# Edge loop of a graph network: VectorE forms the remainder of both message tiles in one operation, and GpSimd issues gathers only

## The reference

```python
edge_feat = concatenate([x[src], x[dst], edge_attr])        # 20000 x 1088
h        = mish(edge_feat @ W1 + b1)                        # 20000 x 512
messages = mish(h @ W2 + b2)                                # 20000 x 512
agg      = segment_sum(messages, dst, num_segments=1250)
```

## Time and profile before

| | |
|---|---|
| time, median of 3 runs | 1254.94 us (1253.52 to 1257.24) |
| the profiled execution | 1255.11 us, span 1253.5 us |
| PE busy in the span | 1084.6 us, 87% |
| DVE busy | 958.0 us, 76% |
| ACT busy | 837.7 us, 67% |
| POOL busy | 713.5 us, 57% |

### The profile page before, as it was taken

The page is one execution under the profiler, slowest core; times in us unless marked ns, Lnnn a source line. Parts: engine busy times, 40 slices in busy tenths (PEclk is TensorE's granted clock), DMA queues, the critical chain, the costliest instruction groups (busy, mean ns, idle before and its releaser), DMA issues. The chain is left out here.

```text
span 1253.5 us, 19768 instructions
## 1 busy us (share of the span) xinstructions
PE 1084.6 (87%) x5651; PEld 884.2 (71%) x5652; DVE 958.0 (76%) x1678; ACT 837.7 (67%) x1025; POOL 713.5 (57%) x574
## 2 busy tenths in 40 slices
PE   3993999999999999999999999996389985668974
PEld 2772788787778778878777877885267764658862
DVE  6651799898989989989989999998548875733366
ACT  3212889989988998998998988897045441523342
POOL 3246777777777777787877777752111210644420
PEclk9995999999999999999999999998589995779985
DMA  6826666666666666666666666660011112624445
GB/s 167 276 89 153 143 121 130 125 125 125 129 126 122 127 128 121 129 126 123 129 125 126 124 126 129 119 149 1 23 46 42 33 58 82 205 76 127 134 130 179
DMA packets 129763, 148.72 MB, mean 119 GB/s; under 512 B 73253, under 2 KB 81862, under 8 KB 129597
## 3 DMA queue, kind: packets, MB, share of 16 engines
q0 software_dynamic: 39280, 97.61, 36.2%
q1 hardware_dynamic: 90381, 50.03, 15.1%
q10 hardware_dynamic: 16, 0.02, 0.0%
HBM read 137.02 MB, written 15.69 MB: 122 GB/s over the span
## 5 line engine op out<-in xcount | busy, mean ns | idle before, releaser
L907 PE MATMUL ps<-W2h,w1l_w3l 128*128 128x512 f32 x1264 | 426.6, 398 | 0.0
L778 POOL DMA_INDIRECT gath<-dst_table,idx_sl x158 | 265.2, 1679 | 48.6 <-issue 47.1
L771 POOL DMA_INDIRECT gath<-src_table,idx_sl x158 | 207.9, 1316 | 126.1 <-PE ps L902 86.0
L907 PEld LDWEIGHTS ps<-W2h,w1l_w3l 128*128 128x128 f32 x1264 | 227.3, 189 | 38.6
L907 PE MATMUL ps<-W2l,w1l_w3l 128*128 128x512 f32 x632 | 248.2, 393 | 0.0
L845 DVE TENSOR_TENSOR agg<-agg,ps 125x512 f32 x166 | 114.0, 687 | 76.5 <-issue 47.7
L785 POOL TENSOR_TENSOR msg_lo<-act,msg_hi 128x512 fp32r<-128x512 f32 x79 | 144.2, 1825 | 35.3 <-DVE msg_hi L891 35.3
L907 PEld LDWEIGHTS ps<-W2l,w1l_w3l 128*128 128x128 f32 x632 | 119.0, 188 | 27.2
L802 ACT ACTIVATE act<-ps 128x1024 f32<-128x1024 f32 x79 | 81.2, 1027 | 74.8 <-PE ps L939 74.8
L902 PE MATMUL ps<-ident,gath 128*128 128x128 f32 x632 | 99.0, 282 | 34.8 <-DVE agg L845 18.4
L902 PEld LDWEIGHTS ps<-ident,gath 128*128 128x128 f32 x632 | 73.6, 142 | 62.5 <-DVE agg L845 35.3
(11 more groups left out here) (324 smaller groups left out, 2391.7 us busy)
## 6 DMA issues: line engine op xcount, KB each, us to landing
f_w_raw<-in_L_ffn_w_dram SPq DMA_DIRECT2D x32, 512.0 KB, 4.7
ea_sl<-ea_scr SPq DMA_DIRECT2D x158, 64.0 KB, 3.2
ea_scr<-in_edge_attr_dram POOLq DMA_DIRECT2D x1, 5000.0 KB
w_raw<-in_L_gnn_W_dram SPq DMA_DIRECT2D x3, 1024.0 KB, 12.6
gath<-src_table,idx_sl POOLq DMA_INDIRECT x158
gath<-dst_table,idx_sl POOLq DMA_INDIRECT x158, 5.1
x_raw<-in_x_dram SPq DMA_DIRECT2D x5, 448.0 KB
src_table<-tabs SPq DMA_DIRECT2D x10, 224.0 KB
```

The source lines that it names most:

```text
L771: pool.indirect_dma_start(out=gath[:, k, j, :], out_offset=None, in_=src_table[:, :], in_offset=bass.IndirectOffsetOnAxis(ap=idx_sl[:, p % ...
L778: pool.indirect_dma_start(out=gath[:, k, j, :], out_offset=None, in_=dst_table[:, :], in_offset=bass.IndirectOffsetOnAxis(ap=idx_sl[:, p % ...
L907: return nc.tensor.matmul(ps_2[:, p % 2, j, :], part[:, p % 2, d, j * P:(j + 1) * P], weights[:, d, :], start=False, stop=last)
```

## The change

VectorE's L867 covers both tiles of the pair (128 x 1024 instead of 128 x 512). GpSimd's subtraction (L785) and its two waits are gone, and two semaphores become one, so ScalarE and TensorE have one wait less each.

```diff
@@ gpsimd
-                p = s - 4
-                if exists(p):
-                    pool.wait_ge(S["msg_hi_ready"], p + 1)
-                    need(pool, S["sum_ps"], ring_free(p))
-                    nc.gpsimd.tensor_tensor(msg_lo[:, ring(p)][:, 1], act2[:, p % A2, 1], f32(msg_hi[:, ring(p)][:, 1]), ALU.subtract).then_inc(S["msg_lo1_ready"], 1)
@@ scalar
-                        act.wait_ge(S["msg_lo0_ready"], g - A2 + 1)
-                        act.wait_ge(S["msg_lo1_ready"], g - A2 + 1)
+                        act.wait_ge(S["msg_lo_ready"], g - A2 + 1)
@@ vector
-                    nc.vector.tensor_tensor(msg_lo[:, ring(m)][:, 0], a4[:, 0], f32(msg_hi[:, ring(m)][:, 0]), ALU.subtract).then_inc(S["msg_lo0_ready"], 1)
+                    nc.vector.tensor_tensor(msg_lo[:, ring(m)], a4, f32(msg_hi[:, ring(m)]), ALU.subtract).then_inc(S["msg_lo_ready"], 1)
@@ tensor
-                    pe.wait_ge(S["msg_lo0_ready"], min(m + 1, PAIRS))
-                    pe.wait_ge(S["msg_lo1_ready"], min(m + 1, PAIRS))
+                    pe.wait_ge(S["msg_lo_ready"], min(m + 1, PAIRS))
```

More of the change, by code:

```diff
@@ L713, in edge_phase @@
         names = ("eaT_ps eaT_hi eaT_lo gath_read lin1_ps exp1 inc1 sq1 ln1 quot1 h_ready h_hi h_lo lin2_ps "
-                 "exp2 inc2 sq2 ln2 quot2 msg_ready msg_hi_ready msg_lo0_ready msg_lo1_ready onehot_ready sum_ps summed w3_in w3_hi w3_lo").split()
+                 "exp2 inc2 sq2 ln2 quot2 msg_ready msg_hi_ready msg_lo_ready onehot_ready sum_ps summed w3_in w3_hi w3_lo").split()
         S = {n: sem("e_" + n) for n in names}
```

## The result

| | before | after |
|---|---|---|
| time, median of 4 runs | 1254.51 us (1253.52 to 1257.24) | 1226.41 us (1225.22 to 1227.05) |
| profiled execution, span | 1253.5 us | 1224.3 us |
| ratio after to before | | 0.9771, 95% interval 0.9754 to 0.9789 |

28 us or 2.3% faster. 1251.5 was forecast, with a range from 1229 to 1268, whose lower end the result misses by 2.6 us. The time is near that of rival A, 1229, but not by rival A's way.

What follows compares the result with a forecast made beforehand. Bound: a per-step ring of 9.46 us through VectorE's register load, held by the adding gather. Sum: 1255.1 - 2.8 (shorter ring) - 1 (last steps) = 1251.3, taken as 1251.5 us; range 1229 to 1268.

Steps and rivals of the forecast that it cites:

- rival A: On GpSimd, first dst gather starts ahead of L879, takes 1.57; load comes later and is free; 1229 us, chance 0.22.
- The held register load: VectorE's load L840 before tile 1's addition takes 1060 ns, not about 310, while the adding gather is on its way.
- the ring: Closed chain each step: bank end, src gathers, first dst gather, load, addition, transposes, bank end; 9.46 us, forecast 9.42.
- the ring law: Step period is first dst gather's end after bank end, plus 2.38, plus 1.40: 5.68 + 3.78 = 9.46 us.
- What moves the gathers: On GpSimd: first src gather 0.44 shorter, first dst gather starts at 3.66; -0.04 us a step, -2.8 us.
- The third gather's length: First dst gather on GpSimd, begun just behind VectorE's L879, takes 2.02 us instead of 1.57 and ends at 5.67.
- rival C: First src gather not shortened or dst gather held longer, ending at 6.12; 1285 us, half of it 1270; chance 0.09.
- The price of 0 for GpSimd's subtraction: Removing L785 moves no gather: 0 us, although GpSimd is busy 148 us less.
- VectorE's part: Doubled L867 adds 0.53 us a step on VectorE, hidden with some 0.35 to spare; 42 us if paid in full.
- TensorE's wait for L875: PE's L910 waits for VectorE's L875 by about 0.1 us each step, with 0.5 to give.
- The last steps: From about 855 us, L785 no longer holds L862, but L867's +0.53 is paid; between -3 and +3, taken as -1.

Runs made afterwards that it cites:

- e3_one_input: Kernel before plus a VectorE reduction (128 x 512, one SBUF input, constant tile) behind L867, GpSimd's subtraction kept: 1270.18 us.
- e8_sub_first: Kernel after with the wide VectorE subtraction moved ahead of L857, so that it ends before the first src gather starts: 1249.62 us.
- e2_pool_to_spare: Kernel after with GpSimd's subtraction put back, its result written to a spare tile that nobody reads: 1259.98 us.
- e1_pool_left_out: Kernel before without GpSimd's subtraction, TensorE multiplying msg_hi in both places, VectorE keeping its 128 x 512 form: 1254.69 us.

## Why the prediction was wrong

**Right: what bounds the kernel.** The held register load and the ring through it stand. Moving the load alone gives the 30 us, and the ring law (end of the first dst gather + 3.74 to 3.78) gives the period of the kernel before, of e3_one_input (9.65) and of e8_sub_first (5.67 + 3.74 = 9.41). It was fitted to the kernel before; the other two are independent of it. Its tacit condition is that the load comes into the transfer; in the kernel after it does not.

**The step that failed: "What moves the gathers", its first term.** I wrote that the first src gather "gets 0.44 shorter" since the CAST moves behind its end. It got 0.41 longer. The 1.43 of before was laid to the CAST L872. e3_one_input shows that it belongs to the subtraction L867, which begins 0.12 ahead of the gather and ends inside it. I took both for explanations of the same 1.43, as the two operations stand back to back. But two rows of before could have separated them. The second src gather of each step (1.29, with L879 beginning 0.48 into it) shows what an operation at the CAST's place gives. And the gather of 0.99 in the earlier trace rows, which I called one with no CAST over it, had L872 (from 613.60 on) over its last 0.33 us and was no longer for it. Made 0.53 longer, L867 holds the gather that much longer: 0.99 + 0.97 - 0.11 = 1.85 against 1.84 measured (from 0.24 ahead to 0.97 inside). The dst gather thus moves from 4.11 to 4.53 instead of to 3.66.

**The third gather's length failed too.** The prediction has it at 2.02 by L879, which stands ahead of it. At 4.53 that operation is over; the gather is lengthened by L887 or L891 (now L881 and L885), which begin after it. No term of the prediction has these two. Without them the gather would end at 6.1 and the load at 6.7 would be held, as in the three steps of 9.60 to 9.65: 70 such steps would have made the kernel slower than before, by some 10 us (an estimate, 70 x (9.63 - 9.48), as if each of these steps could follow another). With them it ends at 6.5 or 7.1 and the load is ahead of its transfer. That is luck: 0.15 us in the start of L881 (1.22 or 1.37 into the gather) decides.

**The rule that I set aside.** I weighed the rule of the Trainium skill (SBUF — State Buffer, Who interferes with whom) that a VectorE operation with two SBUF inputs contends with a GpSimd instruction that reads SBUF. I threw it out by one row, a gather of 0.99 under L867. In that row the gather starts at 612.94 and L867 at 613.00: the gather was first. The same section says that who issues first gets the ports; e2_pool_to_spare shows both orders in one trace, 0.99 with the gather 0.05 ahead and 1.95 with it 0.14 behind. I used that rule for rival A and not for this row. I also drew the wrong end from it: a held gather was priced as a longer ring, +45 us, and put under C with a chance of 0.02, when with the later and longer dst gather the load escapes and the ring opens.

**The price of 0 for GpSimd's subtraction.** It is right for the schedule of before (e1_pool_left_out) and wrong for that of after (e2_pool_to_spare), where L785 would end past the bank end and stand in front of the next gather. "It would cost or give something only where the gathers stood behind it" names the condition; I did not put the new times into it.

**A slip in rival C.** Its 6.12 holds the third gather by L879 at its present place, 4.11. By the prediction's own formula only 0.11 of L879 is left there, which costs nothing, so a first gather that is merely not shortened would have left the ring at 9.46.

**Rival A** has the right consequence, the load free and VectorE's own work as the period, 9.1 forecast and 9.09 measured. Its cause, the gather ahead of L879 and the load after the transfer, is not what happened.

**VectorE's part.** +0.53 is exact (L861 1.22). It was forecast hidden with 0.35 to spare; with the ring gone it is the bound. TensorE's wait for L875 (0.1 forecast) came as 0.26 for the weight load; the matmuls on the two sides of L910 start 0.08 further apart than before (0.55 against 0.47), so the forecast holds for the matmuls. The last steps, forecast at -1, gave +0.2 (from the 76th bank end to the last addition 83.1 us before, 83.3 after). The sum: -1.0 up to the sixth bank end, 70 x (9.095 - 9.479) = -26.9, +0.2, and -1.5 in the phases that the change does not touch: -29.2, the difference of the two spans.

## What to carry to other kernels

When an engine idles on its own queue, look at each register load by itself: its duration can depend on the DMA under way, and moving it to a quiet place (0.3 instead of 1.07 us, 1224.5 us here) got what this change got by accident; the two are not apart by their intervals. When two operations stand back to back in front of a slow one, a row does not say which of them holds it; and a row that shows no interference counts only if the order of start is the one in question. How long such an instruction takes counts as much as when it starts: with the short dst gather the same later start gave steps of 9.6. In a loop that closes on itself, an edit must be priced on the schedule it makes: each of two edits gave nothing and both together 33 us.

## What the runs showed of the hardware that had not been expected

- A TENSOR_LOAD of one number from SBUF into a VectorE register took 0.30 to 0.33 us when it was not held. In the edge loops of all thirteen traces, 499 such loads start 0.35 to 1.4 us after the end of an adding (dst) gather's instruction, with no other gather ended in between: all were held and took 0.40 to 1.10 us, most of them the shorter the later they start. 964 start in the same span after a plain (src) gather, and none took more than 0.33. Loads that start up to 0.3 after an adding gather's end are free. So what holds the load is the transfer that adds. Where in the memory it is held was not tried.
- A src gather's instruction took 0.99 us alone, 1.43 with 0.56 us of a two-input VectorE subtraction left when it starts, 1.84 to 1.96 with 0.97 to 1.09 us left, and 0.99 with the same subtraction begun 0.05 us later than the gather. In the other direction, GpSimd's subtraction held VectorE's one-hot to 0.82 and 1.35 us instead of 0.41.
- A dst gather took 2.02 us with a 128 x 1024 TENSOR_SCALAR begun 0.10 ahead of it, and 1.57 unhindered. Operations of the same kind that begin after the gather hold it as well: with a TENSOR_SCALAR that begins 1.22 into it it ended some 0.09 after that one (1.99) or after the CAST that follows (2.59), and with the TENSOR_SCALAR 1.37 or 1.52 into it it took 1.57. Which of the two operations it waits for, in steps that look alike, was not settled.
